# Cross-attention on one core: in the first batch, score tile 4 is normalised by VectorE instead of ScalarE

## The reference

```python
B, C1, C2, N = (8, 512, 512, 1024)
q = jnp.einsum('bcn,dc->bnd', x1, Wq) + bq
k = jnp.einsum('bcn,dc->bdn', x2, Wk) + bk[:, None]
v = jnp.einsum('bcn,dc->bdn', x2, Wv) + bv[:, None]
attn = jax.nn.softmax(jnp.einsum('bnd,bdm->bnm', q, k), axis=2)
attn_out = jnp.einsum('bcm,bnm->bcn', v, attn)
return attn_out + x1
```

## Time and profile before

| what | value |
|---|---|
| device time, median of 3 runs | 635.49 us |
| lowest and highest of these | 634.87 us, 635.52 us |
| device time of the profiled execution | 635.0 us |
| its span, first to last instruction | 633.2 us |
| TensorE busy in the span | 629.5 us (99%) |
| granted TensorE clock | 1.000 |

### The profile page before, as it was taken

The page is one execution under the profiler, slowest core; times in us unless marked ns, Lnnn a source line. Parts: engine busy times, 40 slices in busy tenths (PEclk is TensorE's granted clock), DMA queues, the critical chain, the costliest instruction groups (busy, mean ns, idle before and its releaser), DMA issues.

```text
span 633.2 us, 13435 instructions
## 1 busy us (share of the span) xinstructions
PE 629.5 (99%) x5318; PEld 590.1 (93%) x5318; DVE 442.9 (70%) x511; ACT 328.2 (52%) x430; POOL 143.3 (23%) x115
## 2 busy tenths in 40 slices
PE   9999999999999999999999999999999999999998
PEld 7888899999999999999999999999999999999986
DVE  6995768847778477794777947778568776597351
ACT  6786535735457345474454653555626547265120
POOL 0332200631007400083000830016300353004100
PEclk9999999999999999999999999999999999999999
DMA  8633426963269532776328762287533974345442
GB/s 334 215 133 83 128 84 181 331 143 111 73 176 324 133 126 82 187 285 166 99 83 204 281 159 89 100 227 260 137 93 114 248 243 114 99 132 133 109 145 81
DMA packets 42758, 102.05 MB, mean 161 GB/s; under 512 B 8176, under 2 KB 10224, under 8 KB 42736
## 3 DMA queue, kind: packets, MB, share of 16 engines
q1 hardware_dynamic: 42736, 101.75, 53.4%
HBM read 51.64 MB, written 16.78 MB: 108 GB/s over the span
## 4 chain that ended last, share of the span: by engine, by line
PE 94%; ACT 2%; SPq 2%; DMA 1%; DVE 1%; issue 0%
PE acc_ps L1158 48%; PE acc_ps L1115 23%; PE s_ps L1080 5%; PE s_ps L1228 4%; PE s_ps L1215 3%; PE acc_ps L1178 3%; PE acc_ps L1353 2%; SPq L298 2%; PE acc_ps L1338 1%; PE s_ps L1082 1%; ACT pt_raw L546 1%; PE acc_ps L1190 1%; PE s_ps L1329 1%; DMA pt_raw<-in_front_dram 1%; ACT pt_raw L552 0%; ACT xs_hi L465 0%
## 5 line engine op out<-in xcount | busy, mean ns | idle before, releaser
L1158 PE MATMUL acc_ps<-pt_hi,vt_hi 64*128 64x512 f32 x960 | 201.5, 386 | 0.2 <-DVE pt_lo L727 0.2
L1158 PE MATMUL acc_ps<-pt_lo,vt_hi 64*128 64x512 f32 x960 | 201.3, 386 | 0.0
L1158 PE MATMUL acc_ps<-pt_hi,vt_lo 64*128 64x512 f32 x960 | 201.3, 386 | 0.0
L1158 PEld LDWEIGHTS acc_ps<-pt_hi,vt_hi 64*128 64x128 f32 x960 | 104.3, 184 | 6.5 <-issue 0.8
L1158 PEld LDWEIGHTS acc_ps<-pt_lo,vt_hi 64*128 64x128 f32 x960 | 104.3, 184 | 5.8
L1158 PEld LDWEIGHTS acc_ps<-pt_hi,vt_lo 64*128 64x128 f32 x960 | 104.3, 184 | 5.8
L1115 PE MATMUL acc_ps<-wv_lo,xs_hi 64*128 64x512 f32 x448 | 95.8, 390 | 0.0
L1115 PE MATMUL acc_ps<-wv_hi,xs_hi 64*128 64x512 f32 x448 | 94.9, 386 | 0.0
L433 POOL TENSOR_TENSOR vt_lo<-vt_lo,v_part 128x64 fp32r<-128x64 f32 x56 | 21.0, 380 | 322.1 <-DVE vt_lo L727 322.1
L558 ACT ACTIVATE probs<-s_ps,negmax 128x1024 f32<-128x1024 f32 x56 | 62.5, 1117 | 54.9 <-DVE negmax L814 54.4
L814 DVE TENSOR_REDUCE negmax<-s_ps 128x1 f32<-128x1024 f32 x64 | 76.7, 1210 | 19.7 <-PE s_ps L1082 18.9
(11 more groups left out here) (140 smaller groups left out, 879.2 us busy)
## 6 DMA issues: line engine op xcount, KB each, us to landing
pt_raw<-blocks SPq DMA_DIRECT2D x240, 128.0 KB, 2.3
stage<-in_x_dram SPq DMA_DIRECT2D x32, 512.0 KB, 6.3
o_sb<-in_x_dram SPq DMA_DIRECT2D x64, 256.0 KB, 3.1
out_dram<-o_sb SPq DMA_DIRECT2D x63, 256.0 KB, 2.1
stage<-in_ctx_dram SPq DMA_DIRECT2D x28, 512.0 KB, 9.0
pt_raw<-in_front_dram SPq DMA_DIRECT2D x4, 512.0 KB, 5.7
v_part<-sums SPq DMA_DIRECT2D x56, 32.0 KB, 1.8
stage<-in_front_dram SPq DMA_DIRECT2D x2, 512.0 KB, 7.6
```

The costliest lines, as they stand in the source:

```text
L1158: mm = nc.tensor.matmul(acc_ps[:, OUT_BANK[group], :], v[rows, m, group * P:(group + 1) * P], p[rows, m, :], start=(swap == 0 and m == 0 a ...
```

## The change

In the first batch tile 4 is scaled by VectorE, directly behind its reciprocal, and no longer by ScalarE. VectorE's function is widened so that it can address the tiles of half 1.

```diff
@@ ScalarE, first batch
             first_exp(4)
             first_exp(5)
             round_x1(1, 2)
-            first_normalise(4)
             first_normalise(5)
             first_exp(6)
             first_exp(7)
@@ VectorE
             def first_normalise(t):
                 inverse(t)
                 dve.wait_ge(s_inv, t + 1)
-                nc.vector.tensor_scalar(probs0[:, t, :], probs0[:, t, :], inv[:, t:t + 1], None,
+                nc.vector.tensor_scalar(first_probs(t), first_probs(t), inv[:, t:t + 1], None,
                                         ALU.mult).then_inc(s_norm, 1)
@@ VectorE, first batch
             first_v_lo(6)
             first_v_lo(7)
-            inverse(4)
+            first_normalise(4)
             inverse(5)
             neg_max(0, 6)
             neg_max(0, 7)
```

## The result

The changed kernel takes 636.32 us (median of 20 runs) against 635.16 us of the kernel before (20 runs): ratio 1.0019, with a 95% interval of 1.0013 to 1.0025. That is 1.2 us more, 0.19%; 0.16% and a time of 636.5 us had been forecast. Twenty runs of each resolve a difference that the three shown before could not.

A forecast was written before the change was run, and what follows sets the result against it. TensorE was taken to bound the kernel, with delays on the first batch's chain paid in full. Turn 7 0.99 us later, added to a median of 635.49, gave 636.5 us; range 635.1 to 637.4, the forecast's own 636.1 to 637.1.

The forecast's parts named there:

- What bounds: TensorE, busy 629.5 of 633.2 us; a delay on the first batch's chain to `pt_lo` reaches the end in full.
- The cap of 0.33 on a gain: At TensorE's start of half 1, a faster chain can give at most 0.33 us.
- The duration: VectorE's scaling of tile 4 waits for GpSimd's running subtraction to end and takes 2.46 us; undisturbed it takes 0.75.
- the rule of the Trainium skill: VectorE and GpSimd share ports, the second standing still throughout the other; taken literally, scaling ends 0.19 us later than forecast.
- GpSimd's third low part: GpSimd's last of three next-batch subtractions ends 0.45 us later, at 51.04, hidden by 5 us before its use.
- The rival by which it goes first: GpSimd's third subtraction precedes VectorE's scaling, which ends 2.36 us later than forecast; 638.8 us in all; 6 in 100.
- The list behind it: VectorE's reciprocals, maxima and turns queued behind tile 4's scaling put turn 7 at 54.90, 0.99 us later.
- The DMA part unchanged: From turn 7, the 16 move issues, last landing, `pt_hi` and `pt_lo` keep their distances; half 1 starts at 71.25.
- The second place: TensorE waits 0.57 us at q for the next batch's low part k = 3, not added to the `pt_lo` wait.
- No obstruction: Rival: VectorE's scaling takes 0.75 us, turn 7 comes 0.72 sooner, TensorE uses 0.33; 635.2 us; 10 in 100.
- Less arrives than is late: Rival: the long DMA issue (1.39 us) may be absent or elsewhere; TensorE loses only 0.24; 635.7 us; 12 in 100.

The follow-up runs named there:

- pool_waits: Changed kernel with GpSimd's second and third low part of the next batch held back until tile 4 is scaled; ratio 0.9997 to the kernel before.
- k3_on_pool: Changed kernel with the next batch's fourth low part made by GpSimd and its high part by ScalarE before scaling tile 5; ratio 1.0013 to before.
- one_port: Changed kernel with VectorE's scaling of tile 4 also summing its result into a spare column, another instruction form; ratio 1.0003 to before.
- before_pool_waits: Kernel before, ScalarE still scaling tile 4, with GpSimd's second and third low part held back until that scaling is done; ratio 1.0002 to before.
- scale_after_max6b: Changed kernel with tile 4's scaling moved behind maximum 6 on VectorE, and turn 4 also waiting for tile 5's scaling; ratio 0.9996 to before.
- tile5_too: Changed kernel with tile 5 also scaled by VectorE, directly behind tile 4; ratio 1.0063 to before.

## Why the prediction was right

- *The time.* 636.5 forecast, 636.32 measured. The base was 635.16 and not 635.49, and the rise 1.16 and not 0.99. That the two times lie 0.2 apart is in part luck: the one error is taken up by the other.
- *What bounds.* Right. A delay on the chain from turn 7 to the first `pt_lo` is paid in full: 1.09 later at half 1, 1.2 (0.8 to 1.6) in the runs. The cap of 0.33 on a gain also fits: pool_waits has turn 7 sooner by 0.8 and a ratio of 0.9997, TensorE having nothing left to wait for. But its interval (0.9988 to 1.0006) reaches from a gain of nearly 0.8 to a loss of 0.4, so the cap is read from the profile and not measured.
- *The duration.* 2.46 forecast, 2.45 measured. Reading it off a place in the loop where the same two instructions meet was enough; the wait ends with GpSimd's running instruction and 0.55 is left behind it, as there (0.56). With the full 0.75 behind GpSimd's instruction, as the prediction read the rule of the Trainium skill, it would have been 2.65.
- *GpSimd's third low part*, 0.45 late: measured 7.58 - 7.13 = 0.45. The rival by which it goes first is out.
- *The list behind it.* Turn 7 was forecast 0.99 later and came 0.86 later. Reciprocal 5 was put at the scaling's end; it starts 0.08 ahead of it, and maximum 6 starts 0.07 and not 0.09 behind it: 0.1 of the 0.13. The mis-sized term is the step from the scaling to maximum 6. The path was not quite the forecast's either: in the chain after, turn 7 follows turn 6, and that follows ScalarE (exponentials, scaling 6), where the forecast had reciprocal 7 and scaling 7. The two paths are tied, since scaling 7 (53.92 to 55.08) is over 0.05 before turn 6 (55.13).
- *The DMA part unchanged.* Off by 0.18, the other way, as one issue took 1.58 and not 1.39. The two errors nearly cancel, which is luck: over the profiled kernels the long issue takes between 1.39 and 1.97 (last section). The sum, 0.99 forecast and 1.09 found, is better than its parts.
- *The second place.* A wait of 0.57 at q was forecast; the gap is 57.58 - 56.95 - 0.23 = 0.40, and 0.13 of the difference is the earlier turn 7. It is not added (k3_on_pool).
- *The rivals.* No obstruction: refuted at the start by the 2.45, and pool_waits shows what it would have been. Less arrives than is late: not so here; all of it arrived. But what speaks for it, the long DMA issue, is real: in one_port it took 0.58 more than before, and a move that started 0.6 sooner left half 1 where it was (70.23 against 70.26 in the time of each span).

## What to carry to other kernels

A short instruction moved to another engine brings that engine's neighbours along: before moving it, look what GpSimd is doing at that moment, and find a place in the trace where the same pair already meets. A fast form that must wait for the neighbour can lose to a slower one that need not (2.45 against 1.28 us), and shifting it by one place in the list can be enough (0.86). Where TensorE waits only 0.33 us in all, there is no more than that to gain, and everything else is risk.

## What the runs showed of the hardware, unexpected

**A pause in SP's DMA issues whose length differs.** In each kernel one of the 16 issues of the move is long. This is the one of one_port, from its chain, followed by what the view of DMA queues has for 58 to 59 us of the same execution:

```profile
54.52 0.57 SPq L299
...
58.30 1.97 SPq L299
...
60.31 0.59 SPq L299
```

```profile
q8 instruction: 1, 0.02, 9.3%
```

A packet of the instruction queue starts with the long issue, within 0.1 us, in all eight profiled kernels.

| kernel | first issue | long issue, which | its start | its length |
|---|---|---|---|---|
| pool_waits | 54.50 | 8th | 58.92 | 1.89 |
| one_port | 54.52 | 7th | 58.30 | 1.97 |
| before_pool_waits | 54.98 | 7th | 58.78 | 1.45 |
| before | 55.14 | 7th | 58.92 | 1.39 |
| scale_after_max6b | 55.31 | 7th | 59.11 | 1.54 |
| k3_on_pool | 55.80 | 6th | 58.96 | 1.43 |
| changed | 56.45 | 6th | 59.60 | 1.58 |
| tile5_too | 58.47 | 7th | 62.26 | 1.67 |

The pause goes along with the move (62.26 in tile5_too, whose move is the latest), but not in step: it is the sixth, seventh or eighth issue, so it is not tied to one instruction of SP. The two kernels that started the move soonest have the longest pause. In one_port the head start of 0.6 us is lost by it (the last issue starts at 65.38, before at 65.43), and half 1 starts no sooner. What the packet carries, and whether the issue waits for it, stays open; there is one execution of each kernel, and no run was made on it.

**The clock after a hole.** In tile5_too a wait of TensorE of 3.0 us was followed by 3.2 us at a granted clock of 0.50. The gaps of 0.40 and 0.88 us in the changed kernel, and that of 1.30 us in k3_on_pool, left it at 1.00. The delay of tile5_too so cost 1.7 us beyond its hole, and the shorter ones cost nothing of the kind.
